# Masked attention with residual layernorm on one core: two column bounds and the last subtractions, high parts and normalise move to VectorE

## The reference

```python
scores = jnp.einsum('nd,md->nm', x, ks)
scores = leaky_relu(scores, 0.2)
scores = jnp.where(adj > 0, scores, -9e15)
attn = softmax(scores, axis=1)
out = layernorm(x + attn @ ks)          # over the last axis, eps 1e-5
```

## Time and profile before

| | us |
|---|---|
| median of 3 runs | 1552.17 (1549.71 to 1552.98) |
| device time of the profiled execution | 1553.51 |
| its span | 1551.4 |
| TensorE busy, VectorE busy | 1509.1, 1501.4 |
| ScalarE busy, GpSimd busy | 1480.0, 1440.4 |
| granted TensorE clock, mean | 0.994 of 2.4 GHz |

### The profile page before, as it was taken

The page is one execution under the profiler, slowest core; times in us unless marked ns, Lnnn a source line. Parts: engine busy times, 40 slices in busy tenths (PEclk is TensorE's granted clock), DMA queues, the critical chain, the costliest instruction groups (busy, mean ns, idle before and its releaser), DMA issues.

```text
span 1551.4 us, 43381 instructions
## 1 busy us (share of the span) xinstructions
PE 1509.1 (97%) x16828; PEld 1419.9 (92%) x16828; DVE 1501.4 (97%) x1808; ACT 1480.0 (95%) x1887; POOL 1440.4 (93%) x1246
## 2 busy tenths in 40 slices
PE   6699999999999999999999999999999999999997
PEld 5499999999999999999999999999999999999987
DVE  6999999999999999999999999999999999999984
ACT  6999999999999999999999999999999999999997
POOL 4999999999999999999999999999999999999996
PEclk8999999999999999999999999999999999999999
DMA  9865656555556655566665555655655655555610
GB/s 352 271 200 191 197 198 203 196 188 195 194 191 190 202 189 196 192 191 196 199 192 191 188 188 188 200 183 188 194 189 189 201 185 189 193 188 189 197 63 8
DMA packets 107131, 296.00 MB, mean 191 GB/s; under 512 B 10800, under 2 KB 40240, under 8 KB 106928
## 3 DMA queue, kind: packets, MB, share of 16 engines
q1 hardware_dynamic: 106928, 293.25, 57.6%
HBM read 289.01 MB, written 4.19 MB: 189 GB/s over the span
## 4 chain that ended last, share of the span: by engine, by line
PE 70%; issue 11%; DVE 9%; ACT 7%; POOL 3%; DVEq 0%; DMA 0%; ACTq 0%; POOLq 0%
PE weighted L806 20%; PE scores L758 10%; PE scores L760 10%; PE scores L759 10%; PE weighted L822 6%; PE weighted L818 6%; PE weighted L820 6%; DVE ring L680 3%; ACT ring L493 3%; DVE running L664 3%; ACT pt_hi L500 2%; DVE ring L650 1%; POOL pt_lo L401 1%; POOL kt_lo L363 1%; ACT xt_hi L468 1%
## 5 line engine op out<-in xcount | busy, mean ns | idle before, releaser
L396 POOL TENSOR_TENSOR ring<-ring,floor 128x768 f32<-128x768 f32 (+1 forms) x498 | 706.2, 1418 | 49.2 <-ACT floor L520 49.2
L401 POOL TENSOR_TENSOR pt_lo<-ring,pt_hi 128x512 f16<-128x512 f32 (+1 forms) x512 | 659.5, 1288 | 17.7 <-ACT pt_hi L500 17.2
L650 DVE SCALAR_TENSOR_TENSOR ring<-adj_sb,scores 128x1024 f32<-128x1024 int32 x512 | 620.2, 1211 | 6.8 <-ACT scores L486 6.4
L486 ACT ACTIVATE scores<-scores,shrink 128x1024 f32<-128x1024 f32 x512 | 553.8, 1082 | 51.5 <-PE scores L760 47.0
L493 ACT ACTIVATE ring<-ring,lift 128x1024 f32<-128x1024 f32 x512 | 583.6, 1140 | 1.6 <-POOL ring L396 1.2
L758 PE MATMUL scores<-xt_hi,kt_hi 128*128 128x256 f16 x2048 | 559.8, 273 | 22.8 <-DVE ring L650 15.2
L760 PE MATMUL scores<-xt_hi,kt_lo 128*128 128x256 f16 x2048 | 560.4, 274 | 0.0
L759 PE MATMUL scores<-xt_lo,kt_hi 128*128 128x256 f16 x2048 | 560.1, 273 | 0.0
L664 DVE TENSOR_TENSOR running<-ring,running 128x1024 f32<-128x1024 f32 x448 | 547.2, 1221 | 0.1
L806 PE MATMUL weighted<-k_rows,ring 128*128 128x129 f32 x3472 | 471.6, 276 | 2.0 <-DVE y L701 1.0
L806 PEld LDWEIGHTS weighted<-k_rows,ring 128*128 128x128 f32 x3472 | 426.6, 192 | 14.1 <-ACT ring L493 8.2
(11 more groups left out here) (76 smaller groups left out, 559.2 us busy)
## 6 DMA issues: line engine op xcount, KB each, us to landing
adj_sb<-in_adj SPq DMA_DIRECT2D x512, 512.0 KB, 3.4
ring<-in_ks_t SPq DMA_DIRECT2D x8, 512.0 KB, 7.3
x_row<-in_x SPq DMA_DIRECT2D x32, 128.0 KB, 3.6
out<-normed SPq DMA_DIRECT2D x32, 128.0 KB, 3.6
x_probe<-in_x_t SPq DMA_DIRECT2D x29, 128.0 KB, 3.5
xt_raw<-in_x_t SPq DMA_DIRECT2D x29, 128.0 KB, 4.4
ring<-in_ks SPq DMA_DIRECT2D x12, 128.0 KB, 7.4
k_rows<-in_ks SPq DMA_DIRECT2D x12, 128.0 KB, 3.8
```

Of the source, the lines that this page charges most:

```text
L396: nc.gpsimd.tensor_tensor(here, here, below, ALU.subtract).then_inc(gap_ready, 1)
L401: nc.gpsimd.tensor_tensor(pt_lo[:, g % PARTS, 0:QUAD - whole, :], ring[:, g % RING, whole:, :], pt_hi[:, g % PARTS, 0:QUAD - whole, :], AL ...
L650: nc.vector.scalar_tensor_tensor(ring[:, g % RING, :, :], adj_sb[:, g % ADJS, :, :], 0.0, scores[:, g % 2, :, :], ALU.is_le, ALU.subtract)\
```

## The change

It has two parts.

At the start, the bounds of ks_t steps 6 and 7 move from ScalarE's sum to VectorE's maximum (slots 4 and 5), the bounds of steps 4 and 5 stay on ScalarE but move to slots 3 and 5, behind the high parts of the slot, and the high parts of units 3 to 7 are made one slot earlier (unit 3 in slot 0 beside unit 2). `most(2)` stays in slot 6.

At the end, GpSimd's share of the subtraction ends with piece 493: pieces 494 to 511 are wholly VectorE's (before: 498 to 511), and 492 and 493 take three sub-tiles of four there. VectorE waits for the spread floor in PSUM and no longer for ScalarE's copy in the last block; that copy is not made. VectorE makes the high parts of the last 8 pieces (504 to 511) in place of ScalarE, and the last block's normalise, as (y - mean) * rstd, so that GpSimd's `shift` falls away there.

```diff
-    MAGNITUDES = (2, 4, 6, 7, 8, 9)
+    MAGNITUDES = (2, 4, 8, 9, 10, 11)
-    LEFT_OUT = GROUPS - 2
+    LEFT_OUT = GROUPS + 2
+    LAST_HIGHS = 8
...
-            return QUAD if g >= ALL - LEFT_OUT else 3 if g >= ALL - GROUPS else min(1 + g % 4, 2)
+            return QUAD if g >= ALL - LEFT_OUT else 3 if g >= ALL - LEFT_OUT - 2 else min(1 + g % 4, 2)
+        def wait_high(eng, g):
+            if g < ALL - LAST_HIGHS:
+                eng.wait_ge(part_hi_ready, g + 1)
+            else:
+                eng.wait_ge(dve_hi_ready, g + 1 - (ALL - LAST_HIGHS))
...
 (GpSimd, low_part)
-                pool.wait_ge(part_hi_ready, g + 1)
+                wait_high(pool, g)
 (GpSimd, deviation)
+                if b == BLOCKS - 1:
+                    return
...
 (ScalarE's loop)
-                if g is not None:
+                if g is not None and g < ALL - LAST_HIGHS:
                     high_part(g)
...
-                if 3 <= s < 6:
-                    bound_ks_t(s + 2, s)
-                if s < 8:
+                if s == 0:
+                    split_ks_t(2)
+                if s == 5:
+                    bound_ks_t(5, 3)
+                elif s < 5:
+                    split_ks_t(s + 3)
+                elif s < 8:
                     split_ks_t(s + 2)
-                if s == 1:
+                if s == 3:
                     bound_ks_t(4, 2)
...
-                b = whole_late(s, AT_SPREAD, 1)
-                if b is not None:
+                b = whole(s, AT_SPREAD)
+                if b is not None and b < BLOCKS - 1:
                     spread(b)
...
-                    if b is not None:
+                    if b is not None and b < BLOCKS - 1:
                         normalise(b, j)
...
 (VectorE, gap)
-                dve.wait_ge(floor_ready, b + 1)
+                if b == BLOCKS - 1:
+                    dve.wait_ge(spread_ready, b + 1)
+                else:
+                    dve.wait_ge(floor_ready, b + 1)
...
+            def high_part(g):
+                dve.wait_ge(prob_ready, g + 1)
+                dve.wait_ge(weighted_ready, g + 1 - PARTS)
+                whole = WHOLE[g % GROUPS]
+                nc.vector.tensor_copy(pt_hi[:, g % PARTS, 0:QUAD - whole, :], ring[:, g % RING, whole:, :])\
+                    .then_inc(dve_hi_ready, 1)
+            def normalise(b):
+                dve.wait_ge(normed_ready, SIDES * b)
+                dve.wait_ge(out_stored[b % 2], 16 * (b // 2))
+                dve.wait_ge(rstd_ready, b + 1)
+                for j in range(SIDES):
+                    nc.vector.tensor_scalar(normed[:, b % 2, j, :], y[:, j, :], neg_mean[:, j:j + 1], rstd[:, j:j + 1],
+                                            ALU.add, ALU.mult).then_inc(normed_ready, 1)
             for s in SLOTS:
+                if 4 <= s < 6:
+                    dve.wait_ge(ks_t_loaded[s + 2], 16)
+                    magnitude(mag_k[:, s + 2:s + 3], ks_t_raw[:, (s + 2) * STEP:(s + 3) * STEP])
+                if s == 6:
+                    most(2)
                 b = whole(s, AT_FINISH)
                 if b is not None:
                     finish(b)
-                if s == 6:
-                    most(2)
                 g = group(s, 0)
                 if g is not None:
                     mask(g)
+                g = group(s, AT_PART)
+                if g is not None and g >= ALL - LAST_HIGHS:
+                    high_part(g)
+                if whole(s, AT_NORMALISE[0]) == BLOCKS - 1:
+                    normalise(BLOCKS - 1)
...
                 if s == 5:
-                    dve.wait_ge(mag_k_bounded, 6)
+                    dve.wait_ge(mag_k_bounded, 4)
+                    dve.wait_ge(mag_step, 6)
```

More of the change, by code:

```diff
@@ L173, in adj_attention_layernorm @@
         dve_gap_ready = sem("dve_gap_ready")
+        dve_hi_ready = sem("dve_hi_ready")
         part_hi_ready = sem("part_hi_ready")
@@ L808, in weigh @@
                                          start=(q == t == j == 0), stop=False, skip_group_check=True)
-                pe.wait_ge(part_hi_ready, g + 1)
+                wait_high(pe, g)
                 pe.wait_ge(part_lo_ready, g + 1)
```

## The result

The changed kernel takes 1547.78 us (median of 15, 1545.53 to 1547.92) against 1552.17 (median of 15 runs of the kernel before beside them, 1549.59 to 1553.99): ratio 0.9972, 95% interval 0.9964 to 0.9979, so 4.4 us faster by the medians. The profiled execution took 1547.7 with a span of 1545.8, against 1553.51 and 1551.4: 5.6 us less. That the profiles differ by more than the medians is part of the finding.

The account below looks back on a forecast made before the run. TensorE and VectorE were taken to share the bound of the main part, which the change leaves alone. Start 2.35, end 3.0 and normalise 0.6 sum to 5.95 us off the median 1552.17, giving 1546.2; range 1543.0 to 1549.5.

Parts of the forecast that it names:

- The start, 2.35 us: First units up to mask(8): moved bounds and earlier high parts bring mask(6) and mask(8) 2.35 us earlier.
- Rival 2: Start: the clock stays high, score(8) takes 1.0 us less, 0.7 us more gained in all, 1545.5; chance 0.2.
- From there to the end of the main part: Main part after mask(8): VectorE is busy without a break, so the start's 2.35 us shift is carried through.
- The collision at 63.90: First minimum of a block on VectorE: its 1.57 us wait while GpSimd subtracts stays, as both engines shift alike.
- The end, 3.0 us: Last pieces: split part of 511 begins at 1540.1 against 1543.10, 3.0 us earlier.
- The 0.79 and 0.43 us that ScalarE waited for TensorE: Exponentials 496 to 504: these waits go because TensorE gets pieces 494 and 495 earlier; 14.86 us against 16.08.
- the high part on VectorE: Pieces 504 to 511: each costs 0.65 us, 0.95 with 768 columns; bounds 0.35 and 2.2.
- The 0.8 us wait in piece 507: End: high part of 507 queues on VectorE, so its low part comes 0.8 us later than TensorE wants.
- the forecast's signs of being wrong: Mask(6) early but not the 300th microsecond; a high part over 1.7 us; exponentials of 508 to 511 waiting for VectorE.
- The normalise: Last block: VectorE begins at 1547.99 and needs about 0.25 us for each of two instructions, 0.6 us earlier.
- rival 5: End: VectorE's high parts and GpSimd's low parts take turns, so only the start and normalise gain, 1549.2; chance 0.12.
- rival 6: End: each high part costs VectorE the full 2.2 us, 1555.7; slower at all from 1.75 us; chance 0.04.

Follow-up runs that it names:

- b0: The kernel before, unchanged, executed and profiled a second time; 1551.29 us.
- b2: The kernel before with 23 idle matmuls in TensorE's idle spells of slots 2, 3, 4, 5 and 7; 1549.87 us, ratio 0.9993.
- e7: The changed kernel with the first minimum of block 1 as two instructions, a copy to PSUM and a minimum; 1546.22 us, ratio 0.9970.
- e3: The changed kernel with the last 8 high parts back on ScalarE; 1548.85 us, ratio 0.9985.
- e4: The changed kernel with subtractions shared with GpSimd as before and ScalarE's copy of the last floor back; 1549.25 us, ratio 0.9988.
- e10: Combined, on the changed kernel: idle matmuls, unit 8's low part on VectorE, block 1's first minimum in two, 494 and 495 shared three to one; 1546.29 us.
- b1: The kernel before with 31 idle matmuls in TensorE's idle spells of slots 2 to 7; 1551.19 us, ratio 0.9996.
- e1: The changed kernel with the end set as before, so only the start changed; 1550.64 us against 1550.38 before, ratio 0.9997.

## Why the prediction was right, and where it was not

**The time.** 1546.2 was forecast and 1547.78 measured, inside the range; 5.95 us forecast, 4.4 measured by the medians, 5.6 between the profiled executions. The moves did what they were said to do, but a good part of the agreement is luck: by the profiles at an undisturbed clock the change is worth 2.7 us, and the other 3 of the 5.6 us lay in the granted clock of the one profile that the forecast was read from.

**The start, 2.35 us.** The schedule was right: `most(2)` 29.87 (29.7 forecast), mask(6) 31.13 (30.9), VectorE without idle time from mask(2). Mask(8) came at 37.77 (37.3 forecast): 0.11 of the difference is from mask(0), 0.12 was lost by mask(6), and 0.22 in score(8), now wholly at 1.2 GHz. But the step "from the median, 1552.17 - 5.95" took a gain read against one execution as a gain over all. That execution had 3.0 us in its start that b0 and b2 don't have, and they are in scores at 1.2 GHz. With the full clock in both, the whole change of the start is worth 0.26 us. The low clock cost the start before 2.99 us (26.34 - 23.35) and the changed one 1.23 (24.32 - 23.09), and that difference is the rest of the 2.02: the changed start has fewer scores on VectorE's path while the clock is low. This, with what is lost again in the main part, is the likely reason why start alone is not told from before. Rival 2 asked whether the clock would stay up after the change, and not whether it does so without it.

**From there to the end of the main part.** Carried, as forecast, less 0.45. This loss belongs to the changed start: the nine profiles that have it take 1367.65 to 1367.94 from mask(40) to mask(510), the four of the kernel before and end alone 1367.26 to 1367.35. At the full clock it takes back all of the 0.26. A part of it, 0.3 us, is at piece 358, where VectorE waits 0.45 us between `recip` and `y`; the changed kernel and start alone have it there, the first-minimum kernel doesn't. I did not find what it is.

**The collision at 63.90.** Kept, as forecast, 2.76 us; by e7 its cause is the two SBUF operands. It also takes back a part of what an earlier mask(8) gains: mask(18) to mask(20) takes 7.02 us in before at 0.50, 7.45 in its second execution, 6.99 in the changed kernel, 7.27 with idle matmuls and 7.59 in e3 and e4. Those two lose 1.4 and 1.6 us against the changed kernel between mask(8) and mask(40), of which this is 0.6. Another 0.75 and 0.82 go at mask(34), in the three-column instruction shown above, which took 1.14 and 1.20 us. In these two and in e10, and in no other profile, the granted clock was at 0.50 for 6.8 us from about 65 us on; that this brought the instruction beside GpSimd's low part is likely and was not tested.

**The end, 3.0 us.** The marks came in the forecast order. The exponentials of 496 begin, counted from mask(510), 1.19 us earlier (1.27 forecast), those of 504 2.50 (2.45). The last `denom`: 4.15 - 0.52 = 3.63 us earlier in place of 3.0. One step held in its number and not in its reason. The 0.79 and 0.43 us that ScalarE waited for TensorE were to go because TensorE would get pieces 494 and 495 earlier. They did go: 14.77 us between those two exponentials, 14.86 forecast. But in b2, b1 and e1, whose end is unchanged, they are gone too (14.79 or 14.80), and TensorE in e1 still waits 1.60 and 0.95 us for those low parts. The waits came with the 3.4 us at 0.50 from 1514.3 on, the lower of TensorE's two levels. So 1.2 of the 3.0 us forecast came true by luck, or at least not for the reason given. The term that was mis-sized is the high part on VectorE: 0.65 us was taken from the nearest row, 0.48 was measured, and 0.61 in place of 0.95 with three sub-tiles. The forecast had put 3.8 us beside a high part of 0.35. The 0.8 us wait in piece 507 shrank to 0.16. Of the sum, 1.27 us of the 3.63 is that fall of the clock, which two of the four profiles of the kernel before have and none of the nine with the end changed in whole or in part. Whether the change prevents it is not shown, since e1 and b2 go without it too. At an undisturbed clock the end's gain is 2.36. One of the forecast's signs of being wrong did come, with little behind it: the exponentials of 511 waited 0.29 us for VectorE's subtraction.

**The normalise.** 0.45 in place of 0.6: VectorE starts at rstd's end and takes 0.60 for both instructions in place of the 0.5 estimated.

**The sum with the clock left out.** 0.26 at the start, 0.4 lost in the main part (1367.35 to 1367.74), 2.35 and 0.45 at the end: 2.7 us. What is measured beyond it, 1.7 of the 4.4 us, would come from the executions of before with a clock at 0.50, at up to 3.0 us in the start and 1.3 in the end. No profile counts how often that happens, but every timed execution has its mean granted clock on record. Of the 74 of the kernel before beside the experiments, the 38 under 1551.1 us all have 0.997 or 0.998, and of the 36 above 28 have 0.996 or less. That agrees with the clock as the cause. It doesn't say where in an execution the clock was low, so this last share is argued and not shown.

**Rivals 5 and 6.** Three of the eight high parts were held up: the first (0.94 us in place of 0.48), one of the pair of 508 and 509, and the last. VectorE's timeline of the changed kernel:

```profile
1530.74 1.31 DVE L728 CAST pt_hi<-ring 128x512 f16<-128x512 f32 x2
...
1534.48 1.41 DVE L728 CAST pt_hi<-ring 128x768 f16<-128x768 f32 x1 [1.14 <-PE scores L866]
```

The last takes 1.41 in place of 0.61 and ends at 1535.89; GpSimd's low parts of 508 to 510 (three from 1531.79 on, 3.69 together) end at 1535.48. The first and the pair overlap GpSimd's low parts of 503 and 507 in the same way. So the turn-taking of rival 5 exists, at 0.4 to 0.8 us a time, but only where a low part of an earlier piece is still running, three times of eight and not all along; and no high part came near the 1.75 us of rival 6.

## What to carry to other kernels

Look at the granted clock of the stretch that a change shortens before its gain is subtracted from a median, and take the profile of the kernel before twice when its times lie in clusters. A change that takes TensorE off the waiting path is worth most in the executions where its clock is down, so on average the clock adds to its plain gain the share of such executions times what the low clock costs more before than after. A wait that disappears is no proof of the reason given for it: see whether it is there in an execution of the old kernel with the clock up. In a drain, such as the end here, put work on the engine that has run out of its own, and look for instructions that wait on another engine's queue only because of what stands ahead of them.

## What was not expected of the hardware

- The same kernel ran its first 40 us with the granted clock at 0.50 from 24 to 28 us in one execution and at 1.00 throughout in another, and took 26.34 and 23.35 us to the same instruction.
- An instruction of VectorE on three columns took 0.89 us in place of 0.38 (106.19 in the combined kernel). GpSimd's low part beside it began at 105.89 and took 1.16, so the two ended together. The same holds in all 14 profiles, three times in each: the instruction took 0.37 to 1.20 us, as much as was left of the low part, and ended 0.02 to 0.03 us behind it. So its 0.38 is a wait too. The one before it in the combined kernel, of integers and on one column, took 0.14 beside the same low part. "SBUF — State Buffer" of the Trainium skill, Who interferes with whom, says that `tensor_scalar` can take the port pair shared with GpSimd; the rows agree with it.
- A copy of 1024 columns from SBUF to PSUM on VectorE took 1.22 us beside a busy GpSimd, with no wait; the high parts, copies from float32 to float16 within SBUF, took 0.48 for 512 and 0.61 for 768. By an estimate from these two, 256 columns cost 0.13 and the fixed part is 0.22; with the same fixed part the copy to PSUM costs 0.25 for 256 columns, about twice as much. "VectorE: DVE Perf Modes" of the Trainium skill, The perf-mode tier table, has twice the rate for float32 copies within SBUF, and Why PSUM operands drop a tier has the plain rate for float32 with a PSUM operand; the rows agree.
